# Decoder layer on one core: the last norm of attention taken apart by batch, and two routing steps at other units

## The reference

```python
    x = x + _L0_xattn_ref(ctx_1024, ctx_1024, _layernorm(x, axis=-1), ...)
    x = x + _L0_ffn_ref(_layernorm(x, axis=-1), ...)

def _layernorm(x, axis=-1, eps=1e-05):
    m = jnp.mean(x, axis=axis, keepdims=True)
    v = jnp.var(x, axis=axis, keepdims=True)
    return (x - m) / jnp.sqrt(v + eps)

def _moe_forward(x3, Wg, W1, b1, W2, b2, Ws1, bs1, Ws2, bs2):
    logits = x @ Wg
    probs = jax.nn.softmax(logits, axis=-1)
    vals, idx = jax.lax.top_k(probs, TOP_K)              # 2 of 8 experts
    weights = vals / (jnp.sum(vals, axis=-1, keepdims=True) + EPS)
    ...
    shared = jax.nn.silu(x @ Ws1 + bs1) @ Ws2 + bs2      # 256 -> 1024 -> 256, every token
    out = out + SHARED_SCALE * shared
```

## Time and profile before

| what | us |
|---|---|
| median of 3 runs | 1123.24 |
| lowest, highest | 1118.74, 1123.26 |
| the profiled execution's own time | 1122.69 |
| its span | 1120.8 |
| PE busy in the span | 1000.5 (89%) |
| DVE busy | 806.4 (72%) |
| ACT busy | 749.5 (67%) |
| POOL busy | 626.9 (56%) |

### The profile page before, as it was taken

One profiled execution on the slowest core, in us unless ns is written; L12 is line 12 of the kernel. 1 busy time (PEld: TensorE's weight loads), 2 busy tenths in 40 slices (PEclk: granted clock), 3 DMA queues, 4 the chain that ended last, 5 costly groups with the idle time before them and its releaser, 6 DMA issues.

```text
span 1120.8 us, 16809 instructions
## 1 busy us (share of the span) xinstructions
PE 1000.5 (89%) x5808; PEld 685.6 (61%) x5808; DVE 806.4 (72%) x954; ACT 749.5 (67%) x1725; POOL 626.9 (56%) x389
## 2 busy tenths in 40 slices
PE   5993998989989898998989898898989798999995
PEld 3542555546555565555555576676767564899995
DVE  6798999999999999999999836576657611211110
ACT  3999999999989899998988422556556431233331
POOL 2002999999999999999999804411110005022122
PEclk9995899999999999999999998899989799899998
DMA  5001334444444434434444303500000008689994
GB/s 187 8 7 56 102 112 112 112 111 111 111 112 112 112 111 112 112 112 112 111 112 109 69 1 113 158 26 29 1 1 2 1 1 309 186 267 328 302 309 116
DMA packets 91118, 125.44 MB, mean 112 GB/s; under 512 B 11641, under 2 KB 84490, under 8 KB 91018
## 3 DMA queue, kind: packets, MB, share of 16 engines
q1 hardware_dynamic: 87130, 120.04, 37.7%
q0 software_dynamic: 3904, 4.33, 2.0%
HBM read 115.93 MB, written 9.23 MB: 112 GB/s over the span
## 4 chain that ended last, share of the span: by engine, by line
PE 39%; DVE 30%; issue 12%; DMA 10%; ACT 7%; another core or an unknown queue 1%; DVEq 0%; POOLq 0%; ACTq 0%
DVE states L1718 19%; PE ps L1210 10%; DMA sums<-y_tile,x_tile 10%; PE ps L1088 5%; DVE states L1696 5%; PE ps L1098 4%; PE ps L1190 3%; PE ps L1316 2%; PE ps L1328 2%; DVE neg_max L1800 2%; PE ps L1464 2%; PE ps L1105 2%; ACT probs L1010 2%; PE ps L1473 2%; PE ps L1527 1%
## 5 line engine op out<-in xcount | busy, mean ns | idle before, releaser
L685 POOL TENSOR_TENSOR states<-states,c_row 128x800 f32<-128x800 f32 x255 | 473.7, 1934 | 90.2 <-DVE states L1718 90.2
L1210 PE MATMUL ps<-states,ident 128*128 128x400 f32 x1024 | 375.2, 509 | 11.4 <-DVE u L1726 11.4
L1210 PEld LDWEIGHTS ps<-states,ident 128*128 128x128 f32 x1024 | 187.3, 193 | 127.6 <-DVE u L1726 12.7
L1718 DVE TENSOR_TENSOR_SCAN states<-sb_decay,ps 128x800 f32<-128x800 f32 x128 | 231.2, 1807 | 5.0 <-ACT sb_decay L924 3.8
L1718 DVE TENSOR_TENSOR_SCAN states<-ps,states 128x800 f32<-128x800 f32 x128 | 229.7, 1795 | 1.1 <-ACT ps L924 1.1
L916 ACT ACTIVATE xT<-xn_tok,xT 100x256 f32<-100x256 f32 x512 | 216.5, 493 | 1.1 <-PE ps L1190 0.9
L924 ACT ACTIVATE ps<-dt,neg_a 128x396 f32<-128x396 f32 x256 | 141.2, 583 | 46.5 <-DVE states L1718 46.0
L1190 PEld LDWEIGHTS ps<-ident,xT 100*128 100x128 f32 x1024 | 97.6, 145 | 104.1 <-issue 87.8
L1190 PE MATMUL ps<-ident,xT 100*128 100x100 f32 x1024 | 115.1, 257 | 43.9 <-DVE states L1718 30.9
L924 ACT ACTIVATE sb_decay<-dt,neg_a 128x396 f32<-128x396 f32 x256 | 144.4, 611 | 1.0 <-DVE states L1718 0.9
L1010 ACT ACTIVATE probs<-ps,neg_max 100x361 f32<-100x361 f32 x128 | 70.9, 560 | 64.5 <-DVE neg_max L1800 63.9
(11 more groups left out here) (225 smaller groups left out, 1252.8 us busy)
## 6 DMA issues: line engine op xcount, KB each, us to landing
c_row<-rows SPq DMA_DIRECT2D x256, 200.0 KB, 3.1
w_tile<-in_w SPq DMA_DIRECT2D x40, 1024.0 KB, 5.1
b_row<-rows SPq DMA_DIRECT2D x32, 200.0 KB, 3.1
ctx<-in_ctxT SPq DMA_DIRECT2D x8, 361.0 KB, 4.3
rows_by_slot<-blank_rows SPq DMA_DIRECT2D x1, 2660.0 KB, 11.7
x_tile<-rows_by_slot SPq DMA_DIRECT2D x20, 133.0 KB, 3.8
win<-in_winT SPq DMA_DIRECT2D x2, 1024.0 KB, 10.3
w_shared<-in_w SPq DMA_DIRECT2D x2, 1024.0 KB, 6.6
```

What stands on the lines that cost most here:

```text
L685: nc.gpsimd.tensor_tensor(st, st, c_row[i % C_SLOTS][:].unsqueeze(1).broadcast_to([P, CP, TQ]), ALU.mult).then_inc(product_ready, 1)
L1210: mm = nc.tensor.matmul(ps[:, j, 0:TQ], ident[:], states[i % RING][:, j * TQ:(j + 1) * TQ], start=(n == 0), stop=(n == N - 1), skip_group_ ...
L1718: nc.vector.tensor_tensor_scan(st, rates, inflows, 0.0, ALU.mult, ALU.add).then_inc(scan_done, 1)
```

## The change

1. The norm's steps become functions of their own (`norm_stats`, `norm_moments`, `norm_variance`, `norm_root`, `norm_apply`). In batch b of attention DVE takes the statistics of batch b - 1 in group 3 and its moments in group 4. In the last batch it takes the variance of seven batches in group 4, and in group 6 (`ROOT_AT`) ACT takes one root for the seven, ahead of its copy of that group's probabilities; DVE scales four batches there and three more behind the loop. Batch 7 has a norm of its own at the end.
2. PE turns the first half (`turn_x3(0)`) ahead of the last heads' projection, and the second half (`turn_x3(1)`) behind unit 1 of the shared expert. DVE instead of ACT copies out the second half.
3. The logits stand after unit 2 instead of 1, the ranks after unit 6 instead of 8, and the exponential behind the silu of the logits' own unit. `hidden` is allocated ahead of the weight tiles.

```diff
-LOGITS_AT, RANKS_AT, ROWS_AT = 1, 8, 13
+SECOND_HALF_AT, LOGITS_AT, RANKS_AT, ROWS_AT = 1, 2, 6, 13
+STATS_AT, MOMENTS_AT, ROOT_AT = 3, 4, H // 2 - 2
...
-            jobs.append((("xn3T", k, q), "a"))
+            jobs.append((("xn3T", k, q), "v" if q else "a"))
...
         def _(act):
...
             def attend_step(b, s):
                 for g in (2 * s, 2 * s + 1):
+                    if (b, g) == (B - 1, ROOT_AT):
+                        root(2 * Q + DIRS * Q + 1, 0, B - 1)
                     copy_probs(b, g)
...
-            for q in range(Q):
-                root(2 * Q + DIRS * Q + q + 1, q * BQ)
-            for q in range(Q):
-                for k in range(KD):
-                    copy_out(("xn3T", k, q), xn3T[:, k, chunk(q)], bank(("xn3T", k, q))[:, 0:TQ])
+            for k in range(KD):
+                copy_out(("xn3T", k, 0), xn3T[:, k, chunk(0)], bank(("xn3T", k, 0))[:, 0:TQ])
+            root(2 * Q + DIRS * Q + 2, B - 1, 1)
...
-                if u == LOGITS_AT + 2:
+                if u == LOGITS_AT:
                     act.wait_ge(shifted_ready, 1)
                     nc.scalar.activation(route["exp"][:], route["shifted"][:], ACT.Exp).then_inc(exp_ready, 1)
...
         def _(pe):
...
-            project_heads(B - 1)
-
-
-            for q in range(Q):
+
+            def turn_x3(q):
                 pe.wait_ge(xn_ready, (1 + DIRS + 1) * B + (q + 1) * BQ)
                 for k in range(KD):
                     turned(("xn3T", k, q), lambda b: rows_src[:, b, tile(k)])
+
+            turn_x3(0)
+            project_heads(B - 1)
...
                 shared_first(u)
+                if u == SECOND_HALF_AT:
+                    turn_x3(1)
                 if u == LOGITS_AT:
...
         def _(dve):
...
+            def norm_root(at, size):
                 nonlocal norms
                 norms += 1
+                cols = slice(at, at + size)
                 dve.wait_ge(std_ready, norms)
                 step(nc.vector.reciprocal(rstd[:, cols], std[:, cols]))
...
             def attend_step(b, s):
+                nonlocal steps
                 for g in (2 * s, 2 * s + 1):
                     copy_probs(b, g)
...
+                    if b > 0 and g == STATS_AT:
+                        dve.wait_ge(x2_ready, b)
+                        norm_stats(b - 1, x_tok[:, b - 1, :])
+                        steps += 1
+                    if b > 0 and g == MOMENTS_AT:
+                        dve.wait_ge(dve_step, steps)
+                        norm_moments(b - 1)
+                        steps += 1
+                    if (b, g) == (B - 1, MOMENTS_AT):
+                        dve.wait_ge(dve_step, steps)
+                        norm_variance(0, B - 1)
+                    if (b, g) == (B - 1, ROOT_AT):
+                        norm_root(0, B - 1)
+                        for j in range(BQ):
+                            norm_apply(j, x_tok[:, j, :], rows_src[:, j, 0:D])
                     if g == GROUPS - 1:
                         invert_mass(b)
...
+            for j in range(BQ, B - 1):
+                norm_apply(j, x_tok[:, j, :], rows_src[:, j, 0:D])
             copy_heads(B - 1)
             normalise_heads(B - 1)
-            norm_x(0, rows_src)
             add_attention(B - 1)
             dve.wait_ge(x2_ready, B)
-            norm_x(1, rows_src)
+            layer_norm(B - 1, [(x_tok[:, B - 1, :], rows_src[:, B - 1, 0:D])])
+            for k in range(KD):
+                copy_out(("xn3T", k, 1), xn3T[:, k, chunk(1)], bank(("xn3T", k, 1))[:, 0:TQ])
```

More of the change, by code:

```diff
@@ L309, in decoder_layer @@
         tile_no = sb("tile_no", [P, TILES], scope=moe)
+        hidden = sb("hidden", [P, FT, T], scope=moe)
         w_tile = [sb(f"w_tile{r}", [P, WP], scope=moe) for r in range(W_SLOTS)]
@@ L317, in decoder_layer @@
         shared_sum = sb("shared_sum", [P, KD, T], scope=moe)
-        hidden = sb("hidden", [P, FT, T], scope=moe)
         cwT = sb("cwT", [EA, T], scope=moe)
@@ L796, in _, with root @@
         def _(act):
-            def root(norm, at):
+            def root(norm, at, size=BQ):
                 act.wait_ge(moments_ready, norm)
-                nc.scalar.activation(std[:, at:at + BQ], var_eps[:, at:at + BQ], ACT.Sqrt).then_inc(std_ready, 1)
+                cols = slice(at, at + size)
+                nc.scalar.activation(std[:, cols], var_eps[:, cols], ACT.Sqrt).then_inc(std_ready, 1)
             def copy_out(key, dst, src, func=ACT.Copy, **how):
@@ L1578, in _, with norm_stats, norm_moments, norm_variance @@
             norms = 0
-            def layer_norm(at, pairs):
+            def norm_stats(at, src):
+                nc.vector.bn_stats(stats[:, at, :], src).then_inc(dve_step, 1)
+            def norm_moments(at):
+                nc.vector.bn_aggr(moments[:, at, :], stats[:, at, :]).then_inc(dve_step, 1)
+            def norm_variance(at, size):
+                cols = slice(at, at + size)
+                nc.vector.tensor_scalar(var_eps[:, cols], moments[:, cols, 1], EPS, None, ALU.add
+                                        ).then_inc(moments_ready, 1)
@@ L1593, in layer_norm, with norm_apply @@
                 dve.wait_ge(std_ready, norms)
                 step(nc.vector.reciprocal(rstd[:, cols], std[:, cols]))
+            def norm_apply(at, src, dst):
+                nc.vector.tensor_scalar(dst, src, moments[:, at, 0:1], rstd[:, at:at + 1],
+                                        ALU.subtract, ALU.mult).then_inc(xn_ready, 1)
+            def layer_norm(at, pairs):
+                nonlocal steps
+                for j, (src, _) in enumerate(pairs):
+                    norm_stats(at + j, src)
+                steps += len(pairs)
+                dve.wait_ge(dve_step, steps)
+                for j in range(len(pairs)):
+                    norm_moments(at + j)
+                steps += len(pairs)
+                dve.wait_ge(dve_step, steps)
+                norm_variance(at, len(pairs))
+                norm_root(at, len(pairs))
@@ L1595, in layer_norm, with norm_x @@
                 for j, (src, dst) in enumerate(pairs):
[L1596 to L1601, removed]
+                    norm_apply(at + j, src, dst)
+            def norm_x(q):
+                layer_norm(q * BQ, [(x_tok[:, b, :], xn_tok[:, b, :]) for b in range(q * BQ, (q + 1) * BQ)])
```

## The result

The changed kernel takes 1110.05 us (median of 4 runs, 1108.97 to 1111.36) against 1122.13 us for the kernel before (4 runs). The ratio is 0.9905, with a 95% interval of 0.9888 to 0.9921: faster by 0.95%, 11 to 12 us.

The account below looks back on a forecast made before the run. Two paths to tile 0's first turn on PE bound it, loads (949.1) and PE's work with its hole (898.5 + 56.0 = 954.5); the later, 4.75 us earlier than before, gave 1118.0 us, range 1111.5 to 1123.5.

Parts of the forecast that it names:

- Statistics inside attention: Norm statistics and moments taken by DVE during attention: hidden behind its wait for ACT's keys, cost nothing.
- The root: Root inside the last attention batch: a cost, PE's last turn 1.6 us later and the projection 3.3 us later.
- End of the logits: Logits' end on PE: 898.5 instead of 901.9, 3.4 us gained, since PE has no gap from 885 on.
- The two ends 898.2 and 901.0: Range forecast for the logits' end; 901.0 is the rival in which PE's clock stays low, 1120.4 us, chance 0.13.
- Ranks 12.2 us behind the logits: Ranks on PE: five fewer half-units put them 12.2 us behind the logits instead of 18.9, never waiting for the picks.
- Path D: Loads' path from the ranks to PE's turn of tile 0: 38.4 us, set by DMA throughput, ending at 949.1.
- Path P: PE's own work from the logits' end to the turn of tile 0: 56.0 us, ending 954.5 with the hole, 946.8 without.
- the hole: On path P, PE stands still 4.97 us for a silu, then runs slow 2.7 us: 7.7 us, forecast to stay.
- The case that came true: Rival "the hole closes": late word misses a silu PE needs, path D decides, 10.1 us gained, 1112.6; chance 0.27.

Follow-up runs that it names:

- The exponential alone: Kernel before with only the routing's exponential moved, behind the silu of unit 2 instead of 3: 1121.66 us, ratio 1.0003 (0.9986 to 1.0019).

## Why the prediction was wrong, point by point

- **Statistics inside attention, nothing: right.** From PE's first keys to the last exponentials it is 182.9 to 183.6 us in five traces without the change and 181.4 to 183.6 in nine with it. The one statistics row of the last batch runs at once behind the maximum.
- **The root, 1.6 us at the last turn, 3.3 at the projection: right in the sum.** Counted from the last exponentials the turn is 1.5 us later and the projection 3.7 (887.16 - 879.89 = 7.3 against 3.6). The switch costs one table load: 879.91 + 1.28, the root at 881.20. The drain that the Trainium skill has behind it (ScalarE: Activation LUTs, What ACT_TABLE_LOAD costs) is not in this trace either. A part that the sum did not have is the clock: it fell at 881 and not at 884, and the last turn took 1.23 us instead of 0.70.
- **End of the logits, 898.5: right, in part by luck.** It is 897.97, but 1.3 of it is the earlier end of attention, so the head gave 2.6 us and not 3.4. The two ends 898.2 and 901.0 hang on when the clock rises, and no run shows the term that gives the earlier one. What the traces show: in the kernel before, the clock rose at 898.0, with PE busy without a gap since 892.8; in the changed one it fell at 881.1 and rose at 891.3, with PE busy without a gap since 883.7. One head is no measure of another here.
- **Ranks 12.2 us behind the logits: right.** 12.4, and 7.7 us behind the picks (`both` at 902.6), so they don't wait. The exponential alone is worth nothing, by its own run.
- **Path D, 38.4 us from the ranks: 1.1 too long.** It measured 37.3. The 38.4 was read to the turn of tile 0, but in the kernel before the rows land at 953.26 + 4.7 = 958.0, 37.2 behind the ranks; the rest is PE, which was ready at 959.3.
- **Path P with its hole, 954.5: this step failed.** I wrote "its cause (full DMAs) stays, and the same units lie in it, so I keep it", and moved the hole along with PE's work. The end of the hole keeps the time of the loads and the scatter: the last late word comes 22.0 us behind the first weight load. That load moved by 10.5 us (928.32 to 917.85), PE's last units only by 5.1, and so the late word came before PE needed the silu. PE's path ended at 947.0, and not at 954.5. The runs show that this is the ranks' doing: PE stands still for 3.3 to 5.0 us in all of the six traces with the ranks behind unit 8, whichever norm they have, for at most 0.4 in the seven with unit 6, and not at all with unit 4. Why the words are late stays open.
- **What the hole was worth.** It took 7.7 us of PE in the kernel before. Closing it there alone would have given 1.3, since the rows landed at 958.0. In the sum for the changed kernel it was worth 954.5 - 949.1 = 5.4 us. The turn of tile 0 came 6.8 before the forecast, at 947.7: 5.4 for the hole, 1.1 for path D, and 0.3 from the logits and ranks.
- **The chances.** The case that came true had 0.27, and its reason was the right one: the late word does not fall on a silu that PE needs. Its time, 1112.6, is 1.2 from the profiled execution's 1111.36. That it is so near is partly luck: 1.3 of earlier attention and 1.1 of path D stand against 0.8 less from the head and 0.2 at the ranks.

## What to carry to other kernels

When two paths end nearly together, first find out which one comes last and by how much, and then move each of them for itself. Ask of every stall which events its start and its end keep time with, and move it with those and not with the engine that suffers it. Here a number that sets where a short step stands in a long loop (the ranks, 3 us of PE) was worth half of the gain, because it moved both paths: 8 MB of loads waited behind it, and the late words moved with them. In this kernel such a step should go as early as its inputs allow, up to the point where the other path decides. Where single runs spread by 1%, measure a step inside the trace, from one event to the next, and in more than one trace: the same instructions took up to 4.6 us more or less.

## What the runs showed of the hardware

- Words of PE to ACT come up to 8 us late, counted from the ends that the trace has for PE's products (the products of unit 14 end at 942.0 in the kernel before, and its silu starts at 950.34), while indirect DMAs of GpSimd are under way beside large loads. The last one comes 3.1 to 3.3 us behind the start of the last scatter DMA in twelve of fourteen traces, whether 8.4, 6.3 or 4.2 MB of weights stand ahead of the rows. No packet of instructions moves in that time. The cause is open.
- The same instructions, from the last exponentials to the logits, took 14.7 us in one execution and 19.3 in another. In the first PE's clock stayed at 2.4 GHz until 894, in the second it fell to 1.2 GHz at 879 and rose at 892.
- With 8.4 MB of weights and a scatter ahead of them, tile 0's rows came 29.4 to 30.0 us behind the first weight load in ten traces of nine kernels, and 26.2 to 26.7 us behind it in three with 6.3 MB.
